# Rows of four neighbouring blocks interleaved: larger pieces of y, x and h0, packing from every fourth column

## The reference

```python
def _L0_gnn_ref(input, A, h0, y):
    adj = A * (y @ y.T)
    row_l1 = jnp.maximum(jnp.sum(jnp.abs(adj), axis=1, keepdims=True), 1e-12)
    return 0.9 * (adj / row_l1 @ input) + 0.1 * h0

def _L1_gnn_ref(h, adj, simlar, W_proj, b_proj, W_gcn, b_gcn):
    sim = jnp.tanh(adj * simlar)                     # simlar is adj itself
    filt = sim * (adj > 0)
    vals, idx = jax.lax.top_k(filt, 350)             # 350 largest of a row
    keep = jnp.arange(350)[None, :] < jnp.sum(filt != 0, axis=1)[:, None]
    new_adj = zeros.at[rows, idx].set(jnp.where(keep, vals, 0.0))
    h2 = jnp.tanh(h @ W_proj + b_proj)
    return jax.nn.relu(new_adj @ (h2 @ W_gcn) + b_gcn)

x = _layernorm(x + _L0_gnn_ref(x, adj, h0, y))
x = _layernorm(x + _L1_gnn_ref(x, adj, adj, W_proj, b_proj, W_gcn, b_gcn))
```

## Time and profile before

| | |
|---|---|
| runs | 477.89, 478.86, 480.38 us; median 478.86 |
| profiled execution | 478.8 us |
| its span in the trace | 477.0 us |
| mean granted clock of TensorE | 0.985 |
| PE busy | 449.3 us (94%) |
| PEld busy | 391.1 us (82%) |
| DVE busy | 378.9 us (79%) |
| ACT busy | 262.7 us (55%) |
| POOL busy | 159.5 us (33%) |
| read from HBM / written | 105.57 MB / 2.56 MB |

### The profile page before, as it was taken

How to read it: one execution, slowest core, us unless ns; L and a number is a source line. 1 busy time by engine, 2 the same in 40 slices (tenths; PEclk the granted TensorE clock), 3 DMA queues, 4 the chain that set the end, 5 groups by cost and what they waited for, 6 DMA issues and landing times.

```text
span 477.0 us, 15332 instructions
## 1 busy us (share of the span) xinstructions
PE 449.3 (94%) x5104; PEld 391.1 (82%) x5104; DVE 378.9 (79%) x1401; ACT 262.7 (55%) x353; POOL 159.5 (33%) x309
## 2 busy tenths in 40 slices
PE   3669999999999999999999999999999999999990
PEld 2448888989998899889998878888888888888880
DVE  5889999999999999999999866566566566566552
ACT  4988999999999999999999826300000000000000
POOL 3012544445555554444555431221221221221220
PEclk9988999999999999999999999999999999999996
DMA  8999999999999999999998000000000000000000
GB/s 267 406 419 418 402 419 393 384 416 417 414 416 416 421 418 422 420 419 421 419 415 326 8 0 1 19 11 17 17 11 17 17 11 17 17 11 17 17 18 10
DMA packets 28254, 108.50 MB, mean 227 GB/s; under 512 B 5401, under 2 KB 18226, under 8 KB 18226
## 3 DMA queue, kind: packets, MB, share of 16 engines
q1 hardware_dynamic: 28226, 108.14, 56.6%
HBM read 105.57 MB, written 2.56 MB: 227 GB/s over the span
## 4 chain that ended last, share of the span: by engine, by line
PE 88%; DVE 5%; DMA 2%; issue 2%; ACT 1%; POOL 1%; POOLq 0%; DVEq 0%; SPq 0%; ACTq 0%
PE acc L492 73%; PE words L443 8%; PE proj_acc L571 3%; PE feat_acc L555 2%; DMA a_rows<-in_adj_dram 2%; DVE a_bits L746 2%; PE xnt_acc L547 1%; DVE g_words L302 1%; POOL pack_half L373 1%; DVE turned L830 1%; ACT count_out L648 1%; DVE x_parts L775 0%; PE gram_acc L475 0%; DVE y_diag L760 0%; DVE same_class L850 0%
## 5 line engine op out<-in xcount | busy, mean ns | idle before, releaser
L492 PE MATMUL acc<-x_parts,turned 128*128 128x257 f16 (+1 forms) x1600 | 195.8, 277 | 0.7 <-DVE x_parts L775 0.7
L648 ACT ACTIVATE count_out<-a_rows,ones 128x2688 bf16<-128x2688 f32 (+1 forms) x80 | 190.0, 2375 | 0.5
L492 PEld LDWEIGHTS acc<-x_parts,turned 128*128 128x128 fp8e4 (+1 forms) x1600 | 157.0, 99 | 25.9 <-DVE x_parts L775 1.2
L492 PE MATMUL acc<-f_parts,turned 128*128 128x257 f16 (+1 forms) x1560 | 175.4, 273 | 0.0
L492 PEld LDWEIGHTS acc<-f_parts,turned 128*128 128x128 fp8e4 (+1 forms) x1560 | 151.2, 97 | 23.2 <-issue 0.4
L746 DVE TENSOR_SCALAR a_bits<-a_rows 128x2688 bf16<-128x2688 f32 (+1 forms) x80 | 116.7, 1459 | 3.3 <-DMA a_rows<-in_adj_dram 2.9
L830 DVE TENSOR_SCALAR turned<-a_words 128x320 uint16 (+1 forms) x305 | 66.9, 233 | 58.7 <-PE acc L492 58.4
L400 POOL TENSOR_TENSOR var_eps<-mean_var,consts 128x1 f32<-128x1 f32 x80 | 18.5, 231 | 272.6 <-DVE mean_var L1036 143.2
L403 POOL TENSOR_TENSOR rstd<-var_eps,consts 128x1 f32<-128x1 f32 x80 | 86.0, 1075 | 6.3
L830 DVE TENSOR_SCALAR turned<-same_class 128x320 uint16<-128x320 uint16 x313 | 71.2, 253 | 0.1
L443 PEld LDWEIGHTS words<-pack,a_bits 128*128 128x128 bf16 (+1 forms) x1600 | 53.6, 96 | 10.3 <-DVE a_bits L746 6.7
(11 more groups left out here) (109 smaller groups left out, 289.9 us busy)
## 6 DMA issues: line engine op xcount, KB each, us to landing
a_rows<-in_adj_dram SPq DMA_DIRECT2D x39, 1344.0 KB, 8.1
a_rows<-in_adj_dram SPq DMA_DIRECT2D x39, 1156.0 KB, 8.6
h_rows<-in_L_gnn_h_dram SPq DMA_DIRECT2D x39, 64.0 KB, 6.1
out_dram<-xn SPq DMA_DIRECT2D x39, 64.0 KB, 1.5
xs<-in_x_dram SPq DMA_DIRECT2D x3, 640.0 KB, 10.0
xs<-in_x_dram SPq DMA_DIRECT2D x1, 512.0 KB, 9.0
y_nat<-in_L_gnn_y_dram SPq DMA_DIRECT2D x1, 304.0 KB, 3.6
a_rows<-in_adj_dram SPq DMA_DIRECT2D x1, 84.0 KB
```

The lines of the kernel that those rows point to most:

```text
L492: mm = pe.matmul(acc[par][0:m, 0:PARTS], bits, parts[:, b, 0:PARTS], start=first and b == blocks[0], stop=last and b == blocks[-1])
L648: act.activation(count_out[0:m, 0:w], a_rows[par][h][0:m, 0:w], ACT.Relu, bias=ones[0:m, 0:1], scale=-HUGE, accum_out=col).then_inc(s_coun ...
```

## The change

Blocks 3 to 38 go in nine groups of four: row 4p + e of the 512 neighbouring rows of a group is row p of the group's block e. Blocks 0 to 2 are a group of three in the same way, and the last block stays. The order of rows in HBM and in the result is what it was.

- y is loaded in pieces of four rows, 256 B, and x in pieces of 2 KB (192 B and 1.5 KB for the first three blocks).
- h0 comes four blocks at a time, one transfer of 256 KB into one of two buffers `h0_rows[slot]` [128, 4, 128]; SP issues it in the step after the group's first block and waits for `s_xh` at n - 4.
- Rows of adj are read one by one as before, but the 128 of a transfer lie four rows apart in place of two; the stores of result rows likewise.
- `pack_rows` reads every fourth column (every third in the first three blocks) where it read every second.
- `HB` is 19 in place of 21, so the halves have 2432 and 2568 columns; x comes in parts of 11, 8, 12 and 9 blocks.
- SP's and POOL's programs use `steps8`, a loop of eight steps, since slots and places within a group repeat after eight. POOL increments one more semaphore in a step.

```diff
-    HB = NB // 2 + 1
+    HB = NB // 2 - 1
...
+    WIDE = N - HB * P
...
-    def rows_in(a, b, par, pair, cols):
+    def group(i, c):
+
+        g = (c - TRIO) // 4 + 1
+        return g % 2, i + g // 2
+
+    def place(c):
+        return (c - TRIO) % 4 if c >= TRIO else c
+
+    def rows_in(a, b, i, c, cols):
 
         if isinstance(b, int) and b == LAST:
             return a[FULL * P:N, cols]
-        if isinstance(b, int) and b == 0:
-            return a[0:P, cols]
-        v = a[P:FULL * P, cols].rearrange("(s p e) c -> e s p c", p=P, e=2)[(par + 1) % 2]
+        if isinstance(b, int) and b < TRIO:
+            return a[0:TRIO * P, cols].rearrange("(p e) c -> e p c", e=TRIO)[b]
+        v = a[TRIO * P:FULL * P, cols].rearrange("(s p e) c -> e s p c", p=P, e=4)[place(c)]
         if isinstance(b, int):
-            return v[(b - 1) // 2]
-        s = pair if par == 1 else pair - 1
-        return v[bass.ds(s, 1), :, :].rearrange("a p c -> p (a c)")
+            return v[(b - TRIO) // 4]
+        return v[bass.ds(i * 2 + (c - TRIO) // 4, 1), :, :].rearrange("a p c -> p (a c)")
 
     def column(b):
 
-        return b * P if b in (0, LAST) else P + (b - 1) // 2 * 2 * P + (b - 1) % 2
+        if b == LAST:
+            return FULL * P
+        return b if b < TRIO else TRIO * P + (b - TRIO) // 4 * 4 * P + place(b)
 
     def spacing(b):
-        return 1 if b in (0, LAST) else 2
+        return 1 if b == LAST else TRIO if b < TRIO else 4
+
+    def steps8(eng, step, lag, first):
+
+        for t in range(first):
+            step(t, t % 2, t // 2, 0, t)
+        count = (FULL - first) // 8
+        with eng.Fori(0, count) as i:
+            for c in range(first, first + 8):
+                step(i * 8 + c, c % 2, i * 4 + c // 2, i, c)
+        for t in range(first + count * 8, NB + lag):
+            step(t, t % 2, t // 2, 0, t)
 
...
         X_HALF = (slice(0, NB // 2), slice(NB // 2, NB))
-        X_PART = [slice(q * (NB // 4) + (q > 0), min((q + 1) * (NB // 4) + 1, NB)) for q in range(4)]
+        X_PART = [slice(0, TRIO + 8), slice(TRIO + 8, HB), slice(HB, HB + 12), slice(HB + 12, NB)]
...
-        h0_rows = [sb(f"h0_rows{p}", [P, F]) for p in range(2)]
+        h0_rows = [sb(f"h0_rows{p}", [P, 4, F]) for p in range(2)]
...
+        def quads_of(a, lo, hi):
+            return a[lo * P:hi * P, :].rearrange("(s p e) f -> p s (e f)", p=P, e=4)
+
+        def quad_view(t, lo, hi):
+            return t[:, lo:hi, :].rearrange("p (s e) f -> p s (e f)", e=4)
...
-            def load_rows(t, par, pair):
...
                     sp.dma_start(a_rows[par][h][0:m, 0:HALF[h].stop - HALF[h].start],
-                                 rows_in(adj, t, par, pair, HALF[h])).then_inc(s_rows[par][h], 16)
-
-            def load_h0(n, par, pair):
-                m = rows_of(n)
-                if not isinstance(n, int) or n >= 2:
-                    sp.wait_ge(s_xh, n - 1)
-                sp.dma_start(h0_rows[par][0:m, :], rows_in(h0, n, par, pair, slice(0, F))).then_inc(s_h0[par], 16)
-
-            sp.dma_start(pair_view(y_nat, 1, FULL), pairs_of(y, 1, FULL)).then_inc(s_in["y"], 16)
-            sp.dma_start(y_nat[:, 0, :], y[0:P, :]).then_inc(s_in["y"], 16)
+                                 rows_in(adj, t, i, c, HALF[h])).then_inc(s_rows[par][h], 16)
+
+            def load_h0(n, i, c):
+
+                par, _ = group(i, c)
+                if isinstance(n, int) and n == LAST:
+                    src, dst = h0[FULL * P:N, :], h0_rows[par][0:TAIL, 0, :]
+                elif isinstance(n, int) and n < TRIO:
+                    src, dst = trio_of(h0), trio_view(h0_rows[par])
+                else:
+                    quad = h0[TRIO * P:FULL * P, :].rearrange("(s p e) f -> s p (e f)", p=P, e=4)
+                    s = i * 2 + (c - TRIO) // 4
+                    src = quad[s] if isinstance(n, int) else quad[bass.ds(s, 1), :, :].rearrange("a p c -> p (a c)")
+                    dst = h0_rows[par][:, :, :].rearrange("p e f -> p (e f)")
+                if not isinstance(n, int) or n >= TRIO + 4:
+                    sp.wait_ge(s_xh, n - 4)
+                sp.dma_start(dst, src).then_inc(s_h0[par], 16)
+
+            sp.dma_start(quad_view(y_nat, TRIO, FULL), quads_of(y, TRIO, FULL)).then_inc(s_in["y"], 16)
+            sp.dma_start(trio_view(y_nat), trio_of(y)).then_inc(s_in["y"], 16)
             sp.wait_ge(s_cleared, 1)
             sp.dma_start(y_nat[0:TAIL, FULL, :], y[FULL * P:N, :]).then_inc(s_in["yt"], 16)
-            load_rows(0, 0, 0)
-            sp.dma_start(xs[:, 0, :], x[0:P, :]).then_inc(s_in["x0"], 16)
+            load_rows(0, 0, 0, 0)
+            sp.dma_start(trio_view(xs), trio_of(x)).then_inc(s_in["x0"], 16)
             for q, part in enumerate(X_PART):
-                lo, hi = max(part.start, 1), min(part.stop, FULL)
-                sp.dma_start(pair_view(xs, lo, hi), pairs_of(x, lo, hi)).then_inc(s_in[f"x{q}"], 16)
+                lo, hi = max(part.start, TRIO), min(part.stop, FULL)
+                sp.dma_start(quad_view(xs, lo, hi), quads_of(x, lo, hi)).then_inc(s_in[f"x{q}"], 16)
             sp.dma_start(xs[0:TAIL, FULL, :], x[FULL * P:N, :]).then_inc(s_in["xt"], 16)
...
+            load_rows(1, 1, 0, 1)
             load_h0(0, 0, 0)
-            load_h0(1, 1, 0)
...
-            def step(t, par, pair):
+            def step(t, par, pair, i, c):
                 if not isinstance(t, int) or t >= 2:
-                    load_rows(t, par, pair)
-                if valid(t - 1) and (not isinstance(t, int) or t >= 3):
-                    load_h0(t - 1, (par + 1) % 2, pair if par == 1 else pair - 1)
-            steps(sp, step, 4)
-
-            def store(t, par, pair):
+                    load_rows(t, par, i, c)
+                if valid(t - 1) and c > TRIO and place(c - 1) == 0:
+                    load_h0(t - 1, i, c - 1)
+            steps8(sp, step, 4, TRIO + 8)
...
+            def store(t, par, pair, i, c):
                 m = rows_of(t)
                 sp.wait_ge(s_result, t + 1)
-                sp.dma_start(rows_in(out, t, par, pair, slice(0, F)), xn[par][0:m, :]).then_inc(s_out[par], 16)
-            steps(sp, store, 0)
+                sp.dma_start(rows_in(out, t, i, c, slice(0, F)), xn[par][0:m, :]).then_inc(s_out[par], 16)
+            steps8(sp, store, 0, TRIO)
...
                 m = rows_of(n)
-                pool.wait_ge(s_h0[par], pair * 16 + 16)
+                slot, turn = group(i, c)
+                pool.wait_ge(s_h0[slot], turn * 16 + 16)
                 pool.wait_ge(s_xh, n)
-                pool.tensor_tensor(h0_part[0:m, :], h0_rows[par][0:m, :],
+                pool.tensor_tensor(h0_part[0:m, :], h0_rows[slot][0:m, place(c), :],
                                    alpha[0:m, :].to_broadcast([m, F]), ALU.mult).then_inc(s_h0part, 1)
...
                     pool.wait_ge(s_xn, t - 3)
+                    pool.sem_inc(s_passed, 1)
                     pool.tensor_copy(at(xs, t - 4, m), xn[par][0:m, :]).then_inc(s_kept, 1)
...
-            steps(pool, step, LAG)
```

More of the change, by code:

```diff
@@ L49, in packed_path @@
     WORDS = P // BITS
-    HB = NB // 2 + 1
+    HB = NB // 2 - 1
+    TRIO = 3
+    WIDE = N - HB * P
     HALF = [slice(0, HB * P), slice(HB * P, N)]
@@ L57, in packed_path @@
     FIRST = 13
-    assert F == P and 0 < TAIL <= 2 * WORDS and C == BITS and FULL % 4 == 3 and FULL > FIRST
+    assert F == P and 0 < TAIL <= 2 * WORDS and C == BITS and FULL % 4 == TRIO and HB % 4 == TRIO and FULL > FIRST
     assert NB * WORDS <= 512 and NB % 4 == 0
@@ L149, in packed_path @@
         y_diag = sb("y_diag", [P, NB // PART, TURN, PART * WORDS], BF16)
-        a_rows = [[sb(f"a_rows{p}{h}", [P, HB * P]) for h in range(2)] for p in range(2)]
+        a_rows = [[sb(f"a_rows{p}{h}", [P, WIDE]) for h in range(2)] for p in range(2)]
         LANES = P // 2
         turned_more = a_rows[0][0][:, 0:NB * LANES // 2].bitcast(U16).rearrange("p (b i) -> p b i", b=NB)
-        a_bits = [sb(f"a_bits{h}", [P, HB * P], BF16) for h in range(2)]
-        count_out = sb("count_out", [P, HB * P], BF16)
+        a_bits = [sb(f"a_bits{h}", [P, WIDE], BF16) for h in range(2)]
+        count_out = sb("count_out", [P, WIDE], BF16)
         turned = sb("turned", [P, 2, NB, LANES], U16)
@@ L272, in turned_at, with trio_of, trio_view @@
             return turned_more if isinstance(n, int) and n == NB + 2 else turned[:, par, :, :]
[L274 to L278, removed]
+        def quads_of(a, lo, hi):
+            return a[lo * P:hi * P, :].rearrange("(s p e) f -> p s (e f)", p=P, e=4)
+        def quad_view(t, lo, hi):
+            return t[:, lo:hi, :].rearrange("p (s e) f -> p s (e f)", e=4)
+        def trio_of(a):
+            return a[0:TRIO * P, :].rearrange("(p e) f -> p (e f)", e=TRIO)
+        def trio_view(t):
+            return t[:, 0:TRIO, :].rearrange("p e f -> p (e f)")
         def gram_bank(g):
@@ L309, in _, with load_rows @@
         def _(sp):
-            def load_rows(t, par, pair):
```

(20 more changed lines are left out.)

## The result

The changed kernel takes 489.82 us (median of 6 runs, 488.93 to 490.98) against 478.75 us of the kernel before; the ratio is 1.0229, with a 95% interval of 1.0207 to 1.0251. It is 11 us slower, where I had forecast no difference and a range that ended at 486 us. Its profiled execution, the slowest of the six at 490.98 us, has a span of 489.2 us, 12.2 us more than that of before.

The account below looks back on a forecast made before the run. TensorE, without gaps at 6.31 us a steady step, was taken as the bound, DMA second at 6.24. All terms were 0 except some 0.4 us won from late landing: 478.8 - 0.4 = 478.4 us, range 475.2 to 486.

Parts of the forecast that it names:

- Item 1: Packing's weight loads from `a_bits` at spacing 4 or 3: cost taken as 0, bounds 0 and +35.1 us.
- rival A: Packing's weight read pays for spacing 4 on TensorE: 496 to 513 us, 500 as one number; chance 0.17.
- Item 2: Halves of 19/21 blocks: casts about 1.42 and 1.50 us, 0.08 us less room, cost 0.
- Item 3: h0 loads by fours: at most 0.08 us of DMA queue a step, 0.05 taken, hidden by TensorE; gain 0.
- Item 4: Larger y and x loads at the start: gain 0, bounds 0 and -0.3 us.
- Item 5: Late adj landing near 70 us: earlier loads remove 0.46 us lost in TensorE's steps, some 0.4 won net.
- Item 6: SP's and POOL's loops of 8 steps, one more POOL semaphore increment a step: cost 0.
- Rival B: DMA becomes the bound through adj rows farther apart and h0 bursts: 481 to 487 us, 483 as one number; chance 0.08.
- Rival C: Earlier landings shorten the half-clock start as well: about 475.5 us; chance 0.10.

Follow-up runs that it names:

- after_s2_lean: Changed kernel with packing at spacing 2 and every second product of the first stage left out; 472.81 us, 0.9884 of the kernel before.
- after_s2: Changed kernel with packing reading every full block at spacing 2, all else of the change kept; 479.31 us, 1.0015 of the kernel before.
- lean pair: Kernel before with every second product of the first stage left out, 472.74 us, set beside after_s2_lean, 472.81 us.
- before_s1: Kernel before with packing reading contiguous columns (spacing 1) instead of spacing 2; 478.23 us in one run.

## Why the prediction was wrong

- **Item 1, the spacing: wrong, and it decides.** The price was 8.3 ns a load, not 0; 1404 loads x 8.3 ns = 11.7 us against 11.1 measured (37 steps of 0.29 us make 10.7). It lay within the bounds that I had set (0 and 25 ns), a third of the way. The step that failed is "I take 0, since the only two spacings that the trace has (1 and 2) cost the same". They do, but both lie under a floor that the lines do not set: by the fitted line the read at spacing 2 would allow 20 ns, at 1 13 ns, and the pitch is 25. Two equal values under a floor say nothing on what comes above it. The row that I had named for rival A, half the clock and a pitch of 27.5 in place of 25.0, could not have settled it: the floor hardly follows the clock, and what lies above it doesn't either.
- The rule that I cited there from the Trainium skill ("Advanced Engine Details and Errata", SBUF Cachelines), two hits on a 16 B line for the full rate, is not what the runs show for weight loads: at spacing 4 each line is hit twice and the pitch is 33.5 ns against 25; above the floor the cost grows with the number of lines. The size of a line, 16 B, agrees with them (128 lines at spacing 8 and at 16, and the same pitch to within 1 ns).
- **Item 2, the halves: right.** Casts take 1.43 and 1.49 us in the timeline of after_s2_lean (1.42 and 1.50 forecast), and after_s2 has a step of 6.32 us.
- **Item 3, h0 by fours: right in its outcome.** SP's wait for `xh` is gone, and nothing of it reaches the end. The 0.05 us a step that I had put on it is shown by no run. The lean pair speaks against a larger one: from 36 to 266 us the DMA engines' share is 0.98 with the old pieces and 0.97 with the larger ones, where 0.8 us of a step of some 6.2 us would be 13%. The Trainium skill ("DMA: Bandwidth & Descriptors", Bandwidth) gives 0.95 us for a 64 KB transfer alone; no run here has one alone, and the lean pair shows no such cost in a full queue.
- **Item 4, y and x: right.** ScalarE waited 0.6 us less for y, and after_s2, which has these pieces too, is no quicker.
- **Item 5, the late landing: wrong in its premise.** The steps near 70 us start at 65.48, 72.26 and 79.04, 6.78 us each, with no long one:

```profile
65.48 2.28 PE L529 MATMUL acc<-x_parts,turned 128*128 128x257 f16 x19
...
72.26 2.28 PE L529 MATMUL acc<-x_parts,turned 128*128 128x257 f16 x19
...
79.04 1.17 PE L529 MATMUL acc<-x_parts,turned 128*128 128x257 f16 x9
```

  6.49 of before and 0.29 for packing make 6.78. But the larger pieces are not shown to be the reason. In before_s1, with the old pieces and the pitch of 25 ns, the same steps start at 62.43, 68.92 and 75.42: 6.49 and 6.50 us, no long one either. The 0.46 us of the earlier trace rows belonged to that one execution, and a term of a forecast should not rest on it. after_s2, which should show it as a gain, has steps of 6.50 and 6.67 us there, and no gain in its time that can be told.
- **Item 6, the loops of eight: right**, as far as after_s2 goes, in which they stand.
- **Rival A** was what happened, at a third of its price: I had put it at 496 to 513 us, between bounds whose upper end (each step of the read twice as long) is neared only from spacing 4 to 8 (33.5 to 61 ns), where lines double and are already the limit. The range's upper end of 486 left it out (and B's own upper end, 487, though the sum of 0.83 counts B in full). **Rival B** did not happen: the loads carry less per second only because TensorE asks later, and in the lean pair rows four apart in HBM pass at 419 GB/s, against 420 for two apart. **Rival C** did not. The 12.2 us between the two profiles are 37 steps of 0.29 (10.7), a start 0.57 us later (first product of the stream at 37.37 in place of 36.80), a first step that is 1.1 us longer beside its packing, less the 0.46 us of the earlier trace rows, and 0.3 us after the first stage. That first step runs at half clock for longer:

```profile
37.37 4.26 PE L529 MATMUL acc<-x_parts,turned 128*128 128x257 f16 x19
42.47 2.84 PE L529 MATMUL acc<-x_parts,turned 128*128 128x257 f16 x21
45.98 1.29 PE L529 MATMUL acc<-x_parts,turned 128*128 128x257 f16 x10
```

  The changed kernel's first step takes 8.61 us and that of before 7.18, but in before_s1, whose pace is that of before, it takes 8.05 us and starts at 35.76. So start and first step vary by about a microsecond between profiles, and what of it belongs to the change is not shown.

No version came out of this that beats both kernels: the changed kernel at spacing 2, which packs columns that do not belong to the block, equals the one before, and packing at spacing 3 (which groups of three would need, 39 = 13 x 3) gave 480.39 us in one run, beside 477.49 for one of the kernel before. An 8-bit `a_bits`, which would halve the lines at spacing 4, was not run here.

## What to carry to other kernels

If two values of a size cost the same, ask whether both hide under something else before extending them to a third, and run the third, wrong columns and all: here that was an edit of six lines. A step that is long in one profile may be that execution's alone. A layout that makes DMA pieces larger is paid by whoever has to read at the new spacing: count the 16 B lines that the busiest engine touches, before and after, and price them. And a gain on the second limit is worth only the distance to the third.

## What the runs showed of the hardware

Back-to-back pairs of a 128-column bf16 weight load and a matmul of 8 columns had a pitch of about 6.7 ns + 0.42 ns per 16 B line that the 128 columns touch in a partition, by a fit to spacings 4 and 8, and in no run less than 25 ns: 25, 25, 26, 33.5, 46.5, 61 and 62 ns at spacings of 1, 2, 3, 4, 6, 8 and 16 elements. Above the floor the pitch did not follow TensorE's clock: in the changed kernel 19 matmuls took 0.81 us at 41.42 us, at a granted clock of 0.50, and 0.75 at 1.00. What is longer is the time to the second matmul (73 ns in place of 26); from the fifth on they start 33 ns apart in both.

```profile
41.42 0.81 PE L480 MATMUL words<-pack,a_bits 128*128 128x8 bf16 x19
```

A cast from float32 to bf16 on VectorE went from 0.58 ns a column at spacing 1 to 0.99 ns (2048 columns) and 1.85 ns (2560 columns) when it read every fourth float32, in one run.
